# A four-layer transformer kernel: where GpSimd does its two additions with the bias rows

## The reference

```
h  = norm(x) * (1 + scale1) + shift1
x1 = x + gate1 * (attention(h) @ Wo + bo)        # 16 heads of 16 features
h  = norm(x1) * (1 + scale2) + shift2
x  = x1 + gate2 * (gelu(h @ W1 + b1) @ W2 + b2)  # 1024 hidden features
```

## Time and profile before

| | before |
|---|---|
| median of 3 runs | 1191.89 us (1191.26 to 1197.49) |
| the profiled execution's own time | 1196.37 us |
| its span in the profile | 1194.6 us |
| busy: PE, PEld, DVE, ACT, POOL | 91%, 72%, 65%, 48%, 14% |
| granted TensorE clock, mean over the span | 0.97 |

### The profile page before, as it was taken

The page is one execution under the profiler, slowest core; times in us unless marked ns, Lnnn a source line. Parts: engine busy times, 40 slices in busy tenths (PEclk is TensorE's granted clock), DMA queues, the critical chain, the costliest instruction groups (busy, mean ns, idle before and its releaser), DMA issues.

```text
span 1194.6 us, 21428 instructions
## 1 busy us (share of the span) xinstructions
PE 1087.3 (91%) x7540; PEld 861.0 (72%) x7540; DVE 777.8 (65%) x2091; ACT 574.1 (48%) x1140; POOL 172.8 (14%) x288
## 2 busy tenths in 40 slices
PE   5789999999999999999999888888888999999895
PEld 4568787788787787877788656555566887877675
DVE  4566677766677666767666656666668766776632
ACT  4235655555553445544445434444445545655441
POOL 3010110110113101101101101111114101101100
PEclk9789999999999999999999888999999999999988
DMA  6632333123344223331233423333344123331200
GB/s 232 187 133 85 108 108 104 61 67 89 107 152 178 73 82 107 108 108 61 70 95 107 134 91 107 108 107 108 108 155 141 56 77 117 116 115 62 80 1 18
DMA packets 102714, 123.20 MB, mean 103 GB/s; under 512 B 8992, under 2 KB 96032, under 8 KB 101600
## 3 DMA queue, kind: packets, MB, share of 16 engines
q1 hardware_dynamic: 102048, 121.73, 32.7%
q10 hardware_dynamic: 576, 0.30, 0.1%
HBM read 85.16 MB, written 35.78 MB: 101 GB/s over the span
## 4 chain that ended last, share of the span: by engine, by line
PE 65%; DVE 14%; DMA 9%; ACT 4%; issue 3%; SPq 2%; POOL 1%; ACTq 1%; DVEq 0%; POOLq 0%
PE dense L1175 13%; PE o_banks L1252 9%; PE s_bank L1199 8%; PE dense L1161 8%; DMA q_stack<-max_t 7%; PE st_bank L1236 5%; PE dense L1106 4%; PE o_banks L1135 4%; PE o_banks L1121 4%; DVE neg_max L802 3%; DVE xn L774 3%; PE o_banks L1260 3%; PE o_banks L1085 2%; ACT probs L610 2%; PE s_bank L1209 1%
## 5 line engine op out<-in xcount | busy, mean ns | idle before, releaser
L610 ACT ACTIVATE probs<-st_bank 128x512 f32<-128x512 f32 (+1 forms) x512 | 264.2, 569 | 173.6 <-PE st_bank L1236 120.5
L802 DVE TENSOR_REDUCE neg_max<-s_bank 128x2 f32<-128x512 f32 x384 | 255.7, 684 | 115.6 <-PE s_bank L1199 113.4
L1199 PE MATMUL s_bank<-k_stack,q_stack 96*128 96x256 f32 (+1 forms) x1024 | 235.7, 321 | 19.5 <-DMA k_stack<-qk_dram 9.8
L1199 PEld LDWEIGHTS s_bank<-k_stack,q_stack 96*128 96x128 f32 x1024 | 171.3, 195 | 61.7 <-DVE neg_max L802 18.6
L1175 PE MATMUL dense<-w_sb,hid 128*128 128x256 f32 x768 | 204.9, 381 | 0.0
L1236 PE MATMUL st_bank<-q_stack,k_stack 98*128 98x512 f32 x384 | 153.7, 474 | 15.7 <-DMA q_stack<-max_t 12.8
L445 POOL TENSOR_TENSOR veps<-mv,eps_c 128x2 f32<-128x2 f32 x65 | 12.6, 195 | 977.3 <-DVE mv L768 864.0
L1252 PE MATMUL o_banks<-probs,v_aug 128*32 128x256 f32 (+1 forms) x2048 | 126.2, 390 | 11.5 <-DVE xg L841 6.6
L1175 PEld LDWEIGHTS dense<-w_sb,hid 128*128 128x128 f32 x768 | 128.9, 189 | 9.6 <-issue 0.4
L598 ACT ACTIVATE hid<-dense,vec 128x256 f32<-128x256 f32 x192 | 80.4, 471 | 108.2 <-PE dense L1161 108.2
L1106 PE MATMUL dense<-ht,w_sb 128*128 128x256 f32 x512 | 127.7, 389 | 3.9 <-ACT ht L552 1.3
(11 more groups left out here) (124 smaller groups left out, 1478.5 us busy)
## 6 DMA issues: line engine op xcount, KB each, us to landing
q_stack<-qk_dram SPq DMA_DIRECT2D x192, 128.0 KB, 2.9
k_stack<-qk_dram SPq DMA_DIRECT2D x96, 256.0 KB, 4.1
par_sb<-par_dram SPq DMA_DIRECT2D x32, 512.0 KB, 5.7
qk_dram<-q_hi SPq DMA_DIRECT2D x32, 256.0 KB, 2.1
qk_dram<-q_lo SPq DMA_DIRECT2D x32, 256.0 KB, 2.1
qk_dram<-k_hi SPq DMA_DIRECT2D x32, 256.0 KB, 2.1
qk_dram<-k_lo SPq DMA_DIRECT2D x32, 256.0 KB, 2.1
w_sb<-w SPq DMA_DIRECT2D x3, 1280.0 KB, 7.6
```

The source lines that it names most:

```text
L610: nc.scalar.activation(probs[p % 4][:, kt, :, q0:N], src, ACT.Exp, scale=SCORE_SCALE[l]).then_inc(p_sb, 1)
L802: nc.vector.tensor_reduce(neg_max[:, qt, 2 * p:2 * p + 2], split3(bank[:]), AX.X, ALU.max, negate=True).then_inc(s_max, 1)
L1199: ins = mm(bank[:, e * N:e * N + k1], q_stack[g.par][0:KB, 2 * p + e, qt * P:(qt + 1) * P].bitcast(F32R), k_stack[g.par][0:KB, p, 0:k1].bi ...
```

## The change

Only GpSimd's program changes, and in it only the order and the waits of `step`. Before, it was power of c's norm, pick, addition for c, (split of W1), wait for the bias rows, power of n's norm, addition for g. Now both powers come first, then a wait until VectorE has written n's and c's normalised rows, a wait for the bias rows, and both additions, one behind the other.

```diff
                     if c.layer != 2:
                         pick(c, 1, mod2_now)
 
-                    addend(c, 1, xg2)
                     if g.reg is None and g.off % B == 1 and g.layer > 0 and HAS_MLP[g.layer]:
                         split_w1(g.layer)
-                wait(pool, par_ld, g.count(16, 16))
                 if n.exists:
+
                     power(n, 0, ln1_mv, ln1_veps, ln1_rstd)
-                else:
+                    wait(pool, xn1_done, n.count(1, 1))
+                if c.exists:
+                    wait(pool, xn2_done, c.count(1, 1))
+                    wait(pool, par_ld, g.count(16, 16))
+                    addend(c, 1, xg2)
                     wait(pool, xg2, c.count(1, 1))
-                    wait(pool, xn2_done, c.count(1, 1))
+                else:
+                    wait(pool, par_ld, g.count(16, 16))
                 addend(g, 0, xg1)
```

More of the change, by code:

```diff
@@ L491, in step @@
                         pick(c, 1, mod2_now)
-                    addend(c, 1, xg2)
                     if g.reg is None and g.off % B == 1 and g.layer > 0 and HAS_MLP[g.layer]:
                         split_w1(g.layer)
-                wait(pool, par_ld, g.count(16, 16))
                 if n.exists:
                     power(n, 0, ln1_mv, ln1_veps, ln1_rstd)
-                else:
-                    wait(pool, xg2, c.count(1, 1))
-                    wait(pool, xn2_done, c.count(1, 1))
+                    wait(pool, xn1_done, n.count(1, 1))
[3 more added lines that the diff above has]
+                    addend(c, 1, xg2)
+                    wait(pool, xg2, c.count(1, 1))
+                else:
+                    wait(pool, par_ld, g.count(16, 16))
                 addend(g, 0, xg1)
```

## The result

| | before | with the change |
|---|---|---|
| median of 17 runs each | 1197.34 us | 1190.2 us |
| ratio to before | | 0.9944, 95% interval 0.9922 to 0.9966 |
| the profiled execution's own time | 1196.37 us | 1197.06 us |
| first second norm, us from the start | 86.93 | 92.77 |
| from the first to the last second norm | 1083.04 us | 1077.89 us |

One of the 17 executions of the unchanged kernel took 4354.08 us; the other 16 have a median of 1197.1 us. The kernel is faster by 0.56%, 6.7 us, with an interval of 4.1 to 9.3 us. The sign was forecast; the time was not. The predicted time of 1180.9 us and the range of 1174 to 1187 us were set from a median of three runs, 1191.89 us. Over 17 runs the unchanged kernel has 1197.34 us, so 5.4 us of the miss of 9.3 us lie in that base. The other 3.9 us are the gain: 7.1 us between the medians (6.7 by the ratio) where 11.0 us were worked out.

What follows compares the result with a forecast made beforehand. TensorE, busy 91%, was taken to bound the kernel, idling where GpSimd's addition delays the second norm. Terms 10.4 - 1.4 + 1.0 + 1.0 = 11.0 us took the median from 1191.89 to 1180.9 us; range 1174 to 1187.

Steps and rivals of the forecast that it cites:

- The hold-up: VectorE's second-norm pair waits for GpSimd's addition beside it; freed, it falls from 1.74 to 0.73 us.
- The estimate of 2.01 us: Length of VectorE's held-up pair by the skill's rule, 1.28 + 0.73; the forecast went by the measured 1.74 instead.
- The step sum of 10.4 us: Earlier first MLP product in 20 steps, limited by TensorE's and ScalarE's idle time: 4.8, 2.6, 3.0 us by block.
- the bound that I had set from TensorE's idle time: Block 1's gain limited to TensorE's wait for the normalised rows, 2.6 us in 7 steps.
- Step 31, +1.0: No a to cover TensorE's 2.73 us idle before the transposes, so the whole excess counts: 1.0 us gained.
- Steps 9 and 25, +1.0: The split's CAST now stands where the addition was; pair about 0.8 us earlier or no shorter, 0.5 us gained each.
- The transfers, -1.4: `k_lo` moves up 0.59 us against TensorE's 0.73, so 0.14 us is lost in half of the 20 steps.
- rival 2: Transfers replace the wait before the second half of the scores; steps 9, 25, 31 and a third gain: 3 to 7 us, 18%.
- The additions, at cost nothing: Both additions, now behind n's first norm, still reach the residuals in time and do not slow VectorE's maxima: cost 0.
- The first norm, taken at 0: It loses its 0.74 us hold-up, but nobody uses this: 0, upper bound 1.9 us.

Runs made afterwards that it cites:

- e5: Kernel before, with the addition for c done twice in a row beside the second norm: ratio 1.0222, 1221.6 against 1194.88 us.
- e4: Changed kernel, with GpSimd's split of W1 in steps 9 and 25 waiting for the second norm's rows: ratio to the kernel before 0.9959.
- e6: Kernel before, with the bias rows loaded at the head of each MLP step from step 2 on: ratio 0.9931, 1186.36 us.
- e7: Changed kernel, with the bias rows loaded at the head of each MLP step from step 2 on: ratio to the kernel before 0.9846, 1174.78 us.
- e8: e7 with the split of W1 in steps 9 and 25 also behind the second norm's rows: ratio to the kernel before 0.9857.
- e9: Kernel before, with the bias rows' load put behind the first load of row maxima on SyncE's queue: ratio 1.008.
- e3: Changed kernel, with the bias rows' load issued behind the row maxima in MLP steps: ratio to the kernel before 0.982, 1172.25 us.
- e10: e3 with the split of W1 also waiting for the second norm's rows: ratio to the kernel before 0.9831.
- e1: Kernel before, with only the addition for g waiting until n's first norm is written: ratio 1.0021.

## Why the prediction missed

Two steps put the time outside the range: the base, 5.4 us too low, and the transfers, for which 1.4 us were taken off where `k_lo` and the first MLP product drift apart by 6.2 us. The terms in turn:

**The hold-up: right.** The pair went from 1.74 to 0.73 us in the 20 ordinary steps and in step 31, and e5 settles the cause. On the rule of the Trainium skill, "SBUF — State Buffer", section "Who interferes with whom", that the later of two such instructions waits for the whole of the earlier: e5 agrees that VectorE waits until GpSimd is done, and for each addition in turn. The estimate of 2.01 us that was worked out from it for the pair is too long. In step 3 of the kernel before the first half of the pair alone has this row:

```profile
159.17 1.42 DVE L774 TENSOR_SCALAR xn<-xg,mv,rstd 128x256 f32<-128x256 f32 x1 [0.33 <-POOL rstd L447]
```

It ends at 160.59, 0.15 us behind the addition (160.44), and e5 has 0.16 us; free, such a half takes about 0.4 us. So not all of it was still to be done when the addition ended.

**The step sum of 10.4 us: a little low.** Measured between the second norm and the first MLP product it is 100.0 - 88.0 = 12.0 us: 5.1, 3.7 and 3.2 us for blocks 0, 1 and 3, where 4.8, 2.6 and 3.0 were taken. Only in block 1 did it pass the bound that I had set from TensorE's idle time, 2.6 us in 7 steps. The bound was too small. Step 10, before and with the change:

```profile
416.90 0.66 PE L1085 MATMUL dense<-ident,xn 128*128 128x128 f32 x4 [0.33 <-DVE xn L774]
```

```profile
420.98 0.37 PE L1236 MATMUL st_bank<-q_stack,k_stack 98*128 98x256 f32 x1
421.19 0.60 PE L1089 MATMUL dense<-ident,xn 128*128 128x128 f32 x4
```

The norm starts at 415.11 and 419.88, so the transposes moved from 1.79 to 1.31 us after it, by 0.48, where the bracket had 0.33. The bracket counts from the end of the product ahead; when nothing holds the transposes they start 0.16 us before that end (420.98 + 0.37 = 421.35). ScalarE does the same in this step: it moved by 0.52 us, where its bracket had 0.40. An idle time in a bracket is thus a bound only when this overlap is added to it. A new wait of 0.1 to 0.3 us for the low part was expected and is there: eight new ones, 2.0 us in all.

**Step 31, +1.0: 0.7 came.** TensorE's idle time fell by 2.73 - 1.75 = 0.98 us, as forecast. But 0.24 us of it was lost again where the additions, now later, held up the CAST of the same path; the prediction had looked for such a meeting only at the maxima and the residuals.

**Steps 9 and 25, +1.0: nothing came.** The step said that the pair would end earlier unless the subtraction behind the CAST came ahead of its second half. It did: the pair lasts until the subtraction ends. The later CAST, which "may move either way", gave back 0.74 us in each step, and the subtraction behind it took 0.67 us of that. The stretch to the MLP went from 13.00 to 12.95 us in the two steps together. e4 shows that the split can be kept off, for 2.1 us in the norm.

**The transfers, -1.4: the step that failed.** The prediction let `k_lo` move up 0.59 us against 0.73 for TensorE, from step 3 alone. Over the 20 steps `k_lo` moved from 1.66 to 1.37 us after the start of the norm, by 0.29 us, while the first MLP product moved up by 12.0 / 20 = 0.60. The limit is the one that the step names, the end of `k_hi`; but in step 3 that end lay early (1.07 us after the start of the norm, against a mean of 1.27). All the loads of stacks and row maxima stand behind the store of `k_lo`. If they bound TensorE in all 20 steps, 20 x 0.31 = 6.2 us would be lost. The waits for the row maxima grew by 2.0 us in these steps, inside the 0.2 us a step that the prediction allowed; the 1.3 us more for the stacked keys it had not named.

What was lost can be read from the table, with care. The transfers take 210.8, 204.8 and 207.2 us in the three profiles in which the addition stands beside the second norm, a mean of 207.6. They take 214.6, 211.2 and 219.6 us in the three in which it doesn't, a mean of 215.1. That is 7.5 us more, with a scatter of 6.0 and 8.4 us within the two threes. With the rows moved, the difference is 2 to 5 us (e6 to e7 and e8) and 2 us (e9 to e3 and e10). So the loss is 2 to 7.5 us, and 12.0 + 0.7 less that is 5 to 11 us, with the measured 6.7 in it.

The start of `k_lo` is a better mark. From there to the second half of the scores the 20 steps take 277.6, 271.7 and 277.3 us in the same first three profiles (mean 275.5), and 275.3, 271.9 and 280.3 us in the second three (mean 275.8). Behind `k_lo` nothing changed that can be seen, so by this the ordinary steps gained what `k_lo` did, 20 x 0.29 = 5.8 us, and with step 31 it is 6.5 us. That agrees with the measured 6.7; with a scatter of 6 and 8 us inside each three it is no proof. That `k_lo` moves less than TensorE is measured; that this is the whole of the loss was not tested by itself. This is rival 2 in its mechanism, and at 6.7 us in its size of 3 to 7 us too, though in the norm itself all steps gained, not a third of them.

**The additions, at cost nothing: right but for the 0.24 us in step 31.** The maxima of 128x512 keep 0.69 us, beside GpSimd's work too, the residuals 0.69 and 0.86 us as before, and VectorE never waits for the sums. In block 2 both are there by 756.8 us, with the second residual at 760.57. The first norm, taken at 0, can't be told from 0 by e1.

**The base.** I took the median of three runs as the level and subtracted from it. The range of the three reached 1197.49 us, and the profiled execution lay at 1196.37: both spoke for a level several us higher, and I kept the lower one. The level itself is no better than a few us: the three later sets, of 29, 17 and 11 executions, have 1194.3, 1194.9 and 1194.6 us for the same kernel.

## What to carry to other kernels

When one engine's work is taken from beside another's, list every chain that starts there (here the transposes, and the store of the low keys) and measure over all steps how far each can move: the gain is what the slowest of them gives. A reordering may also matter by a dependency that it removes: with the wait for the bias rows gone from GpSimd's power, their 512 KB load could go behind the 8 KB loads that TensorE waits for, and that made the kernel with the lowest median of the study, 1172.25 us, 1.8% under the kernel before. It is not the only way: e7 moves the load ahead of the small ones instead, which the old order allows too, and can't be told from e3. Executions scatter by several us from start-up, transfers and block 2, so a level wants more than three runs, and two profiles are compared by the parts of a step.

## What the runs showed of the hardware that was not expected

- **A hold-up is per instruction, not per pair.** The first instruction of VectorE's pair waits for the addition (1.42 of the 1.74 us, step 3 of the kernel before); the second runs free unless another GpSimd instruction has started by then. So 0.61 us of CAST with a subtraction right behind costs as much (2.09 us) as an addition with a CAST behind it (2.03 us).
- **Other instructions are held too.** Beside the split VectorE's CAST of 128x512 takes 0.79 to 1.55 us instead of 0.43, and its subtraction with both inputs in SBUF 0.98 to 1.65 us instead of 0.69. Maxima that read PSUM keep 0.69 us.
- **The place of a 512 KB load in the queue is worth as much as the hold-up.** With it moved from between the stacked keys and the row maxima, to either side, the transfers part is 12 to 20 us shorter in 20 steps than the mean of the same order of GpSimd (12 and 14 for e6 and e9, 14 to 20 for the others), against 12.0 us for the norm. By the time, e6 gains 0.69% and the change 0.56%.
- **The start-up alone scatters by 11 us.** The first second norm began between 83.1 and 94.5 us in twelve profiles. The stretch before it has a mean granted clock of 0.87 in the earliest and 0.71 in the latest. Windows of e9, and of e5 (busy times, then PEclk, DMA share and GB/s):

```profile
32.00:83.00 51.00, 42.37 (x244) 29.96 (x244) 30.54 (x71) 16.54 (x33) 3.12 (x6) 0.87 0.50 165
```

```profile
32.00:94.00 62.00, 51.47 (x242) 37.45 (x242) 30.18 (x71) 16.18 (x33) 2.76 (x6) 0.71 0.40 131
```

TensorE has about the same number of products in both stretches (244 and 242), and is busy 9.1 us longer in the second, at more of the lower of its two levels of clock (1.2 and 2.4 GHz). Right behind it both stand at 1.00. Block 2 is the other stretch with less than the full clock, see the text below the table.
